# Attention with relative positions: own heads masked and summed for two units at once, relative values moved behind the copy for the maximum

## The reference

```python
content = jnp.einsum('bhqd,bhkd->bhqk', q, k)
relative = jnp.einsum('bhqd,qkd->bhqk', q, rpk)
scores = (content + relative) / jnp.sqrt(jnp.float32(hd))
w = jax.nn.softmax(scores, axis=-1)
out = jnp.einsum('bhqk,bhkd->bhqd', w, v) + jnp.einsum('bhqk,qkd->bhqd', w, rpv)
out = out.transpose(0, 2, 1, 3).reshape(B, S, D)
return out @ Wo.T + bo
```

## Time and profile before

| what | us |
|---|---|
| median of 3 runs (464.59 to 465.99) | 465.7 |
| the profiled execution: its own time | 468.0 |
| the profiled execution: its span | 466.2 |
| busy in the span: ScalarE | 414.7 |
| busy in the span: TensorE | 402.2 |
| busy in the span: VectorE | 396.3 |
| busy in the span: GpSimd | 314.8 |

### The profile page before, as it was taken

One profiled execution on the slowest core, in us unless ns is written; L12 is line 12 of the kernel. 1 busy time (PEld: TensorE's weight loads), 2 busy tenths in 40 slices (PEclk: granted clock), 3 DMA queues, 4 the chain that ended last, 5 costly groups with the idle time before them and its releaser, 6 DMA issues.

```text
span 466.2 us, 24907 instructions
## 1 busy us (share of the span) xinstructions
PE 402.2 (86%) x10258; PEld 335.8 (72%) x10258; DVE 396.3 (85%) x887; ACT 414.7 (89%) x806; POOL 314.8 (68%) x370
## 2 busy tenths in 40 slices
PE   0888888688999999999999999999999999999863
PEld 0345554477888887878888888878878888888652
DVE  8879766558888899989999899999999999999774
ACT  2889999559999999999999999999999999999710
POOL 6557786617575767777777777777777777777510
PEclk9999999979999999999999999999999999999987
DMA  8724744873112525425242524253442515245885
GB/s 151 224 64 125 125 92 130 159 144 80 26 39 56 76 58 96 74 68 84 56 95 51 82 51 80 66 73 75 80 72 66 93 42 93 53 80 94 170 184 170
DMA packets 159528, 43.09 MB, mean 92 GB/s; under 512 B 122320, under 2 KB 156600, under 8 KB 159288
## 3 DMA queue, kind: packets, MB, share of 16 engines
q1 hardware_dynamic: 152304, 40.19, 42.6%
q10 hardware_dynamic: 7112, 1.31, 1.8%
HBM read 21.55 MB, written 16.79 MB: 82 GB/s over the span
## 4 chain that ended last, share of the span: by engine, by line
ACT 42%; issue 20%; PE 14%; DVE 3%; POOL 0%; ACTq 0%; DVEq 0%; POOLq 0%
ACT big L1201 21%; ACT s L1159 11%; ACT ps_y L1181 4%; ACT xr L1166 4%; ACT p L1181 3%; PE ps_s L1030 3%; PE ps_s L1025 2%; DVE mx L1240 2%; PE ps_t L1117 2%; PE ps_s L1129 2%; PE ps_s L1107 1%; PE ps_r L1071 1%; PE ps_o L1047 1%; PE ps_r L252 1%; POOL big L871 0%
## 5 line engine op out<-in xcount | busy, mean ns | idle before, releaser
L871 POOL TENSOR_TENSOR big<-p,big 128x512 f16<-128x512 f32 x128 | 148.4, 1159 | 99.1 <-ACT big L1201 98.3
L1284 DVE TENSOR_REDUCE mcol<-ps_t 128x4 bf16<-128x512 bf16 x128 | 87.8, 686 | 29.1 <-PE ps_t L1117 28.9
L1030 PE MATMUL ps_s<-by_q_room,e 96*128 96x64 f16 x2048 | 103.9, 192 | 0.7 <-issue 0.3
L1025 PE MATMUL ps_s<-qbd,kst 96*128 96x128 f16 x1024 | 99.6, 219 | 3.2 <-PEq L300 2.5
L1244 DVE TENSOR_TENSOR big<-ps_y,big 128x512 f16<-128x512 f32 x128 | 87.5, 684 | 6.7 <-ACT big L1201 6.5
L1240 DVE TENSOR_TENSOR mx<-s,ps_s 128x512 bf16<-128x512 bf16 x128 | 86.7, 678 | 3.2 <-ACT s L1159 2.1
L1030 PEld LDWEIGHTS ps_s<-by_q_room,e 96*128 96x128 f16 x2048 | 85.6, 97 | 1.5 <-issue 1.5
L1159 ACT ACTIVATE s<-ps_s 128x512 bf16<-128x512 f32 x128 | 79.6, 622 | 7.2 <-PE ps_s L1030 7.0
L1201 ACT ACTIVATE big<-p 128x512 f16<-128x512 f32 x128 | 83.5, 652 | 0.0
L276 POOL COPY by_q_room<-qrel 96x256 uint32<-96x256 uint32 x128 | 79.2, 635 | 3.4 <-POOLq L300 3.1
L1181 ACT ACTIVATE ps_y<-ps_s 128x512 f32<-128x512 f32 x128 | 76.1, 594 | 5.7 <-PE ps_s L1129 4.3
(11 more groups left out here) (110 smaller groups left out, 532.7 us busy)
## 6 DMA issues: line engine op xcount, KB each, us to landing
rel_dram<-xr SPq DMA_DIRECT2D x32, 256.0 KB, 2.9
xr<-rel_dram SPq DMA_DIRECT2D x60, 128.0 KB, 3.7
kst<-big SPq DMA_DIRECT2D x48, 64.0 KB, 2.0
qrel<-qr_dram SPq DMA_DIRECT2D x192, 16.0 KB
qbd<-q_dram SPq DMA_DIRECT2D x192, 16.0 KB
y_dram<-big SPq DMA_DIRECT2D x4, 512.0 KB, 2.8
big<-y_dram SPq DMA_DIRECT2D x4, 512.0 KB, 5.7
out<-big SPq DMA_DIRECT2D x8, 256.0 KB, 3.2
```

The lines of the kernel that those rows point to most:

```text
L871: nc.gpsimd.tensor_tensor(probs[:, k // 8, 1, 1, k % 8, :], p32[:, k % 2, 1, :], probs[:, k // 8, 0, 1, k % 8, :], ALU.subtract).then_inc( ...
L1025: nc.tensor.matmul(bank[:, P * g:P * g + P], kst[:, g, S * k + P * kh:S * k + P * kh + P], rhs, start=(g == 0), stop=False, skip_group_che ...
L1030: ins = nc.tensor.matmul(bank.rearrange("p (h q j) -> p h q j", q=Q0, j=J)[:, :, q, :], e4[:, first:first + P], rhs.rearrange("p (h j) -> ...
L1284: nc.vector.tensor_reduce(mcol[:, k % 2, :], ps_tb, X_AXIS, ALU.max).then_inc(mcol_ready, 1)
```

## The change

Mask and sum work on pairs of units. The products of an even unit go to columns 0 to 127 of `ps_o`, those of the odd unit behind it to columns 128 to 255. In odd steps n, behind the maximum `mx`, `own_pair` masks units n-3 and n-2 in one operation of 256 columns, and `sum_pair` right behind it sums both. The step thus waits for the product of unit n-2, which TensorE computes in the same step n. Even steps have neither. `own_ready` and `out_summed` count pairs, so the waits on them are halved. On ScalarE `move_relative` goes from behind the exponentials to behind `copy_half`.

```diff
--- before.py
+++ after.py
@@ -873,7 +873,7 @@
 
             def add_high(m):
 
-                pool.wait_ge(out_summed, 8 * (m + 1))
+                pool.wait_ge(out_summed, 4 * (m + 1))
                 pool.wait_ge(land_in[m % 2], 16 * LOADS * (m // 2 + 1))
                 nc.gpsimd.tensor_tensor(block_of_att(m), block_of_att(m), landed(m, 0), ALU.add).then_inc(att_hi_added, 1)
 
@@ -1039,12 +1039,13 @@
                 pe.wait_ge(lo0_ready, n + 1)
                 pe.wait_ge(lo1_ready, n + 1)
 
-                wait(pe, own_ready, n)
+                wait(pe, own_ready, n // 2)
+                room = slice(P * (n % 2), P * (n % 2) + P)
                 for kh in range(KH):
                     for x, low in ((0, 0), (1, 0), (0, 1)):
                         for g in range(G):
                             val = v_sb[:, KH * k + kh, g, VD * low:VD * low + VD]
-                            ins = nc.tensor.matmul(ps_o[32 * g:32 * g + 32, 0:P], val, probs[:, k // 8, x, kh, k % 8, P * g:P * g + P],
+                            ins = nc.tensor.matmul(ps_o[32 * g:32 * g + 32, room], val, probs[:, k // 8, x, kh, k % 8, P * g:P * g + P],
                                                    start=(kh == 0 and x == 0 and low == 0), stop=(kh == KH - 1 and low == 1),
                                                    skip_group_check=True)
                 ins.then_inc(pv_ready, 1)
@@ -1098,7 +1099,7 @@
                     pe.wait_ge(exp_ready, ALL)
                 if m == 2:
                     pe.wait_ge(mcol_ready, ALL)
-                    pe.wait_ge(own_ready, ALL)
+                    pe.wait_ge(own_ready, ALL // 2)
                 wait(pe, last_ready, (0, 2 + 2 * bg)[qh])
                 for half in range(2):
                     wait(pe, y_sum_ready, 2 * (m - 3) + half + 1 if m == 3 else 0)
@@ -1205,15 +1206,15 @@
                 for k in range(UNITS):
                     if unit(qb, k - 1):
                         exponentials(*unit(qb, k - 1))
-                    rel = relative_of(qb, k, 13)
-                    if rel:
-                        move_relative(*rel)
                     if unit(qb, k - 1):
                         high_part(*unit(qb, k - 1), 0)
                     if k < UNITS - 1:
                         copy_half(qb, k + 1)
                     elif not last:
                         copy_half(qb + 1, 0)
+                    rel = relative_of(qb, k, 13)
+                    if rel:
+                        move_relative(*rel)
                     if unit(qb, k - 1):
                         high_part(*unit(qb, k - 1), 1)
 
@@ -1244,22 +1245,23 @@
                 nc.vector.tensor_tensor(probs[:, k // 8, 1, 0, k % 8, :], ps_y[:, :],
                                         probs[:, k // 8, 0, 0, k % 8, :], ALU.subtract).then_inc(lo0_ready, 1)
 
-            def own_heads(qb, k):
-
-                n = UNITS * qb + k
-                dve.wait_ge(pv_ready, n + 1)
-
-                wait(dve, out_summed, n - 1)
-                nc.vector.tensor_tensor(own[:, k % 2, :].rearrange("p (q h) -> p q h", h=HH), ps_o[:, 0:P].rearrange("p (q h) -> p q h", h=HH),
-                                        hmask[:, :].rearrange("p (o h) -> p o h", o=1).to_broadcast([P, QN, HH]),
+            def own_pair(qb, k):
+
+                pair = (UNITS * qb + k) // 2
+                dve.wait_ge(pv_ready, 2 * pair + 2)
+                wait(dve, out_summed, pair)
+                nc.vector.tensor_tensor(own[:, :, :].rearrange("p s (q h) -> p (s q) h", h=HH),
+                                        ps_o[:, 0:2 * P].rearrange("p (q h) -> p q h", h=HH),
+                                        hmask[:, :].rearrange("p (o h) -> p o h", o=1).to_broadcast([P, 2 * QN, HH]),
                                         ALU.mult).then_inc(own_ready, 1)
 
-            def sum_heads(qb, k):
-
-                dve.wait_ge(own_ready, UNITS * qb + k + 1)
-                if qb == 0 and k == 12:
+            def sum_pair(qb, k):
+
+                dve.wait_ge(own_ready, (UNITS * qb + k) // 2 + 1)
+                if qb == 0 and k == 13:
                     dve.wait_ge(nat_out[1], 64)
-                nc.vector.tensor_reduce(attT[:, k, QN * qb:QN * qb + QN], own[:, k % 2, :].rearrange("p (q h) -> p q h", h=HH),
+                nc.vector.tensor_reduce(attT[:, k - 1:k + 1, QN * qb:QN * qb + QN],
+                                        own[:, :, :].rearrange("p s (q h) -> p s q h", h=HH),
                                         X_AXIS, ALU.add).then_inc(out_summed, 1)
 
             def denominators(m, piece):
@@ -1290,8 +1292,6 @@
                                                 v["x_sb"][:, own, :], ALU.add).then_inc(rest_added, 1)
                         dve.wait_ge(rest_added, 1)
                         nc.vector.memset(ps_r[:, :], 0.0).then_inc(rel_zero, 1)
-                    if unit(qb, k - 3):
-                        own_heads(*unit(qb, k - 3))
                     if unit(qb, k - 1):
                         low_part(*unit(qb, k - 1))
                     if k < UNITS - 1:
@@ -1302,8 +1302,9 @@
                         m = stage_at(qb, k, (25 + piece, 26 + 2 * piece))
                         if m is not None:
                             denominators(m, piece)
-                    if unit(qb, k - 3):
-                        sum_heads(*unit(qb, k - 3))
+                    if k % 2 and unit(qb, k - 2):
+                        own_pair(*unit(qb, k - 2))
+                        sum_pair(*unit(qb, k - 2))
             maximum(0, 0)
             loop(dve, body)
 
@@ -1314,7 +1315,7 @@
                 sums = block_of_att(m)[:, x]
                 for piece in range(2):
                     denominators(m, 2 * half + piece)
-                dve.wait_ge(out_summed, 8 * (m + 1))
+                dve.wait_ge(out_summed, 4 * (m + 1))
                 nc.vector.tensor_tensor(sums, sums, landed(m, 0)[:, x], ALU.add).then_inc(last_hi_added, 1)
                 dve.wait_ge(last_hi_added, done)
                 nc.vector.tensor_tensor(sums, sums, landed(m, 2)[:, x], ALU.add).then_inc(last_lo_added, 1)
@@ -1332,15 +1333,11 @@
                     nc.vector.tensor_tensor(y_v[:, qh, b0:b0 + 4, :], banks[m][half].rearrange("p (b n) -> p b n", b=4),
                                             y_v[:, qh, b0:b0 + 4, :], ALU.add).then_inc(y_sum_ready, 1)
 
-            own_heads(NQB - 1, UNITS - 3)
-            sum_heads(NQB - 1, UNITS - 3)
             low_part(NQB - 1, UNITS - 1)
-            own_heads(NQB - 1, UNITS - 2)
-            sum_heads(NQB - 1, UNITS - 2)
             for piece in range(4):
                 denominators(BG * NQB - 3, piece)
-            own_heads(NQB - 1, UNITS - 1)
-            sum_heads(NQB - 1, UNITS - 1)
+            own_pair(NQB - 1, UNITS - 1)
+            sum_pair(NQB - 1, UNITS - 1)
             add_rest(0)
             for half in range(2):
                 finish_half(BG * NQB - 2, half)
```

## The result

The change made the kernel a little faster, by a third of what was forecast. Over 17 runs of each the median went from 465.72 to 463.88 us; the ratio of the runs is 0.9955, with a 95% interval of 0.9935 to 0.9974. That is 2.1 us of 466 (1.2 to 3.0), where 6.7 were forecast, and the median lies just above the range of 456.6 to 463.8. The profiled execution of the changed kernel took 463.45 us with a span of 461.6.

A forecast was written before the change was run, and what follows sets the result against it. ScalarE, VectorE and TensorE were nearly full, no single bound from shares. 28 groups x 0.22 = 6.2 us plus 0.5 from the first steps made 6.7, taking the median from 465.7 to 459.0, range 456.6 to 463.8.

The forecast's parts named there:

- What bounds the kernel, and the method: Three engines nearly full, no single bound from shares; start-to-start times and waits walked over four steps and a move, 10.62 us before.
- Part (b): VectorE's odd steps: mask and sum of a pair cost 0.79 us, the wait for same-step products 0.05; step 2.64.
- The two rivals in which the odd step is dearer: VectorE's pair about 1.0 us eats the gain, 465.3 (chance 0.13); above 1.01 VectorE becomes the bound, about 479 (0.07).
- The weighing of the page: VectorE's sum behind its mask: the page says semaphores cost nothing extra, sum 0.12 us sooner; the prediction followed the rows instead.
- Part (e): The sum over all steps: 6.2 us from 28 groups, some 0.5 from the steps before moves begin, 6.7 in all.
- The walk behind the move: VectorE's low part in the move step starts 3.57 us behind mcol; its 0.20 idle there was to go.
- Part (d): Walk over four steps and a move: ScalarE's own 10.32 us plus 0.08 lost, 10.40 against 10.62, a gain of 0.22.
- ScalarE never waits: Rival: with the pair 0.08 us cheaper or more, four steps take ScalarE's own 10.32, giving 456.8 us; chance 0.14.
- Part (c): Move behind the copy ends 0.96 us later; delays to TensorE's relative products and SyncE's loads for GpSimd costed at nothing.
- The last steps and the tail: In the tail the last pair is 0.3 us dearer, but VectorE later idles 2.98 for a transfer, so nothing.

The follow-up runs named there:

- sum_first_old_move: Changed kernel with a second buffer for masked heads, the older pair's sum ahead of the next mask, and the move in its old place: 462.87 us, ratio 0.9916.
- rel_only: The kernel before with only the move of relative values put behind the copy, masks and sums per unit as before: 466.31 us, ratio 0.9993.
- the swap: On SyncE's queue the 12 loads of relative queries go ahead of the store: 466.15 us in the kernel before, 462.86 us in the changed kernel.
- after_last_early: Changed kernel with the swap, and the five moves of the last block of queries in their old place: 462.44 us, ratio 0.9906.
- sum_last_early: after_last_early with a second buffer for masked heads, the older pair's sum ahead of the next mask: 461.71 us, ratio 0.9883 to the kernel before.

## Why the prediction was wrong

Right were these:

- *What bounds the kernel, and the method.* Undisturbed groups were walked to 10.62 before and 10.40 after; the trace has 10.62 and 10.46. The two halves alone, walked the same way before they ran, are 10.53 and 10.52, and measured 10.53 and 10.53.
- *Part (b), the pair's price.* 0.79 forecast, 0.80 measured, and the wait for the products 0.05 forecast, 0.06 measured. The two rivals in which the odd step is dearer fall.
- *The weighing of the page.* In the changed kernel the sum, which waits for the 256-wide mask, starts 0.46 behind it. In sum_first_old_move, what follows an equally wide mask without a wait on it starts 0.33 behind. What the Trainium skill (VectorE: DVE Perf Modes, The DRAIN you can't avoid) measured on eight `tensor_copy`, that the semaphore costs nothing extra, is not so for this pair: here the wait cost 0.13 us. The same section says that a next operation that is not held starts earlier, and that is what the 0.33 shows.
- *Part (e), the first steps.* 0.5 us forecast; steps 2 to 13 took 27.64 us, against 28.11 before, 0.5.
- *The walk behind the move.* Its low part comes 3.57 behind mcol; measured are 3.58 (235.22 to 238.80). But the prediction also said that no idle would stand before this low part, against its own walk, where VectorE is free at 3.25. The trace has 0.24 of it.

Two slips changed no result: of ScalarE's six distances from 247.53 to 250.46 the prediction lists one 0.48 too many (0.50, 0.47, 0.48 and 1.48 make the 2.93), and from step 13 to 121 there are 27 groups, not 28.

Wrong were three terms, in the order of their size:

1. *Part (d), 28 x 0.22 = 6.2 us.* It is 27 x 0.16 = 4.3 us, 1.9 less. ScalarE's floor of 10.32 was put together from one stretch without a pause, 2.93 less 0.48, read from start to start just behind a wait. The same rows have the right figure from end to end: the exponential of 247.53 lasts 0.58 and that of 250.46 lasts 0.63, so the ends are 2.98 apart, and less 0.48 that is 2.50 a step. When nothing ever waits the floor is 10.44 (sum_first_old_move), above the 10.40 that the walk gave. The rival "ScalarE never waits" could for this reason not come true at 456.8 us. Part (d) also left out that scores wait for the exponential that reads their bank. That wait ends 23 weight loads in the list, but costs little, as ScalarE is the bound: what all waits together add to its own 10.44 is 0.02 a group.
2. *Part (c), SyncE's queue, costed at nothing.* It cost about 1.6 us. The step was that the slack of 3.6 us "shrinks to 2.7" and that GpSimd "would absorb most of a 0.9 us delay". The slack was read in one stretch, where the 12 loads took 4.52 us to issue; in the long case above they took 5.62, and it was 1.7. The trace of the kernel before has such a turn itself: the loads from 271.1 us on took 5.93 to issue, and the copy started 2.2 behind the last. How long they take to land stood in no row. And GpSimd's idle share did not help, as its next subtraction was due for TensorE's products. Behind them VectorE now stands still too, the coupling that part (b) named and priced for the undisturbed step alone; but rel_only, without this coupling, lost as much.
3. *The last steps and the tail, costed at nothing.* From step 121 to 127 the changed kernel took 17.5 and 18.0 us, the kernel before 16.8 and 16.4 and, with the swap that did nothing, 17.4; the tail was 29.5 and 29.2 against 28.9, 28.1 and 28.5. That is 0.9 and 0.8 us in the mean, with a scatter as large. The cause is open: with the five moves of the last block back in their place the last steps took as long. The table says more of the tail. In the five profiles with the old place it is 28.0 to 28.9 us, in the six with the late move 29.0 to 29.5, with the pair or without it, so it goes with the move. The time lies in the transfers. SyncE issues its last two loads of `y_dram`, 512 KB each, 3.5 to 4.3 us behind the last mcol in the first five and 4.4 to 5.0 in the other six, and the last loads of relative values, which wait for the last store, follow at 11.3 to 12.7 and at 12.3 to 12.9. With the five moves back these are 3.7 and 12.0 in after_last_early, but 5.5 and 13.4 in sum_last_early. That the later large loads hold up the last store fits all of these; no run tried it.

The sum with the first two corrected is 4.3 + 0.5 - 1.6 = 3.2 us, against 2.1 measured. The changed kernel with the swap gained 3.8 us where groups and first steps give 4.8. Both leave 1 us for the third term, which is no better known than that. These terms come from a profile or two or from differences of times, each uncertain by about 1 us, so such a sum is a check and no proof.

The baseline was no part of the error. The profiled execution of the kernel before was 2.3 us long for its kind, as the prediction said, and a second one was short (span 462.3), with the same groups. But the comparison of the two first profiles alone, 466.2 and 461.6, would have made the gain 4.6 us. Only runs side by side show the 2.1.

## What to carry to other kernels

When an operation is moved later on its engine, follow everything that it releases through the queues, the transfers behind it included, and ask for the smallest slack over all turns of the loop, not for the one in the stretch that was read; an idle share does not absorb a delay. Take the floor of a busy engine from end to end as well as from start to start: where the durations grow along the stretch, the starts alone read it too low. Best is a stretch in which it never waits, and where there is none the floor is an estimate. A wait for work of the same step also passes on every irregular pause of the other engine, and a second buffer that lets the older result be taken first removed the wait of the sum for the mask, and in the undisturbed step also that of the mask for the products.

## What the runs showed of the hardware

Five back to back operations of ScalarE took 2.47 to 2.50 us from end to end, in every kernel. From start to start they read 2.46 behind a wait, while their recorded durations grow by some 0.03 us a step (0.60, 0.63, 0.66), and 2.48 to 2.49 once these stay near 0.68. VectorE's 256-wide mask from PSUM lasted 0.42 us, where the 128-wide one took 0.28 to 0.29: 1.05 ns for each further element, as taken from the 128-wide and 512-wide rows. The sum of 256 elements lasted 0.42, that of 128 elements 0.29 behind a mask that it waits for the earlier trace rows and 0.23 where it does not the earlier trace rows. Single executions of one kernel differ by up to 1%, 463.6 to 468.2 us in 17 runs, and the profiles show pauses of TensorE at changing places that no semaphore ends, such as this one of the changed kernel in the last steps:

```profile
425.91 0.51 PE L1072 MATMUL ps_r<-big,gv 128*24 128x128 f16 x23 [0.69 <-issue]
```

Whether these pauses are all of the difference was not tried.
